# Splitting the eight PSUM banks two, four and two in a pairwise attention body

## The chip, the cores and the metric

One Trainium2 chip; the program runs on one core. The time is the device time of one execution, in microseconds (us). A core has TensorE (PE in the profile, its weight loads PEld), VectorE (DVE), ScalarE (ACT), GpSimd (POOL) and SyncE (SP), which each take their own instructions in order and meet at semaphores. TensorE writes its products to PSUM, which has eight banks of 128 partitions x 512 fp32 values.

## The reference, cut to what matters

The program is a four-layer network on x of 8 x 512 tokens x 256 features; each layer is an attention and a feed-forward part, each added to x. Three of the four attentions (layers 0, 2 and 3) have 16 heads of 16 features and use the code that is changed here. Layer 2 shows what is computed:

```python
q = (query @ Wq.T + bq).reshape(B, Tq, H, D).transpose(0, 2, 1, 3)
k = (key @ Wk.T + bk).reshape(B, Tk, H, D).transpose(0, 2, 1, 3)
v = (value @ Wv.T + bv).reshape(B, Tk, H, D).transpose(0, 2, 1, 3)
scores = jnp.einsum('bhqd,bhkd->bhqk', q, k) * SCALE
attn = jax.nn.softmax(scores, axis=-1)
out = jnp.einsum('bhqk,bhkd->bhqd', attn, v)
out = out.transpose(0, 2, 1, 3).reshape(B, Tq, C)
return out @ Wo.T + bo
```

Layer 0 has a mask that hides keys (an integer mask, 1 or 0), layer 3 a mask of floats that is added to the scores. Layer 1's attention and all feed-forward parts are other code, which the change leaves alone.

## The kernel before

The stages run one after another. `attention_by_pairs` makes one attention. It first projects queries, keys and values (`resident_projections`), and then runs the **body**, which the change is about. Tiles of the three attentions carry the same names in the profile (a_psA, a_psS, a_psZ, a_pT). The three bodies are called body 0, body 2 and body 3 below, by their layer.

The body works on pairs of heads. The two heads of a pair lie on partitions 0 to 63 and 64 to 127 of the stacks `qs` and `ks`; `par` is 0 or 1 and says which. There are 8 batches x 16 heads / 2 = 64 pairs, and a pair takes four steps, so a body has 256 steps (`QUARTERS`). A group is two pairs, 8 steps (`STEPS`); a batch is four groups, 32 steps. In each step t TensorE issues, in this order and by hand:

- body 0 only: two products of 512 columns that put the mask's term into the banks of `psS` (`hide_keys`, L1465, called H here);
- **A** (`maxima_scores`, L1455): the scores of 128 queries against all 512 keys, one product for each head of the pair, into `psA`. They are for step a = t + 16 (`LEAD`), two groups ahead. VectorE takes from each the largest score of each query (**R0** for par 0, then **R1** for par 1; L1663 in bodies 2 and 3, L1659 with a mask in body 0) and increments `a_used` with each;
- **S** (`exp_scores`, L1477): the scores the other way round, 128 keys by 512 queries, one product for each head, into `psS`. The maxima enter it as extra rows of the stack. ScalarE takes the exponential of each into `pT` (L1591) and increments `exp_done` with each;
- **Z** (`values`, L1492): pT times the values of the pair before, 8 instructions (16 records), into `psZ`;
- at some steps one piece of further work that uses a free bank of `psZ`: the transpose of the negated maxima (L1506, once in a group), four transposes of the finished heads (L1519, once in a group), four transposes of a batch's output (L1527, twice in a batch), a quarter of the output product (L1535, four times in a batch), and in body 0 eight products for masked rows (L1514, four times in a batch).

VectorE has two further duties among its reductions: `split_maxima` once in a group, and `take_output` once in a group, in the step after L1519, which it waits for before it goes on to R0 and R1 of that step.

The eight banks of PSUM are divided three, three and two: `psA`, `psS`, `psZ`. The products of `psA` and of `psS` use their three banks in rotation, by `unit(t, par)` = 2t + par, modulo 3. One wait stands ahead of each pair of products:

```python
if a >= 1:
    pe.wait_ge(a_used, 2 * a - 1)       # A: the pair starts when R0 of the step before is done
...
if t >= 1:
    pe.wait_ge(exp_done, 2 * t - 1)     # H and S: when the first exponential of the step before is done
```

Ahead of the 256 steps stand 16 steps with A alone, and the last 16 steps have no A.

Of the kernel before, what the change touches and what calls it, by code (L numbers as in the profile page):

```python
# [6 lines left out]
ACT = mybir.ActivationFunctionType  # L7
# [5 lines left out]
AX_X = mybir.AxisListType.X  # L13

P = 128
B = 8
S = 512
D = 256
N_TOK = B * S
TB = S // P  # L20
# [1007 lines left out]
HIDDEN = -1e30  # L1028
# [205 lines left out]
def attention_by_pairs(nc, A, G, nm, w, q_scale, hidden=None, added=None):  # L1234
# [9 lines left out]
    ring = 4 if hidden is not None else 5  # L1244
    with ExitStack() as ctx:
# [3 lines left out]
        psum = lambda n, s, d=F32: ctx.enter_context(nc.psum_tensor(nm + n, s, d))  # L1249
# [127 lines left out]
        mx = sb("mx", [P, 2, 2, 2, TB])  # L1377
# [3 lines left out]
        oh = sb("oh", [P, GH, P])  # L1381
        rden, on = sb("rden", [P, GH, TB]), sb("on", [P, 2, TB, D])
        oT, osb = sb("oT", [P, KD, S]), sb("osb", [P, 2, 2 * D])
        psA, psS, psZ = psum("psA", [P, 3, S]), psum("psS", [P, 3, S]), psum("psZ", [P, 2, S])
        a_ready, s_ready = [sem("a_ready0"), sem("a_ready1")], [sem("s_ready0"), sem("s_ready1")]
        a_used, max_ready, exp_done, o_done, oh_ready, rden_ready, x_full, x_free = (
            sem(n) for n in ("a_used", "max_ready", "exp_done", "o_done", "oh_ready", "rden_ready", "x_full", "x_free"))
# [32 lines left out]
        def unit(t, par):  # L1420
            return 2 * t + par

        with nc.Block() as block:
# [21 lines left out]
            def _(pe):  # L1445
                def maxima_scores(a):
                    p, q = a // TB, a % TB
                    g = p // 2
                    if a % STEPS == 0:
                        pe.wait_ge(group_loaded[g % ring], 16 * LOADS * (g // ring + 1))  # L1450
                    if a >= 1:
                        pe.wait_ge(a_used, 2 * a - 1)
                    for par in range(2):
                        r = slice(64 * par, 64 * par + max_row)
                        nc.tensor.matmul(psA[:, unit(a, par) % 3], qs[r, g % ring, p % 2, q * P:(q + 1) * P], ks[r, g % ring, p % 2],  # L1455
                                         start=True, stop=True).then_inc(a_ready[par], 1)

                def hide_keys(t):
                    u, kt = t // (TB * H // 2), t % TB
                    if t % (TB * H // 2) == 0:  # L1460
                        pe.wait_ge(hide_k_ready, u + 1)
                    if t >= 1:
                        pe.wait_ge(exp_done, 2 * t - 1)
                    for par in range(2):
                        nc.tensor.matmul(psS[:, unit(t, par) % 3], G.identb[:], hide_k[:, u % 2, kt, :], start=True, stop=False,  # L1465
                                         skip_group_check=True)

                def exp_scores(t):
                    p, kt = t // TB, t % TB
                    g = p // 2  # L1470
                    if t % STEPS == 0:
                        pe.wait_ge(max_stored[g % 2], 32 * (g // 2 + 1))
                    if t >= 1:
                        pe.wait_ge(exp_done, 2 * t - 1)
                    for par in range(2):
                        r = slice(64 * par, 64 * par + ROWS)
                        nc.tensor.matmul(psS[:, unit(t, par) % 3], ks[r, g % ring, p % 2, kt * P:(kt + 1) * P], qs[r, g % ring, p % 2],  # L1477
                                         start=(hidden is None), stop=True, skip_group_check=True).then_inc(s_ready[par], 1)

                def values(t):  # L1480
                    p, i = t // TB - 1, t % TB
                    g, par = p // 2, i // 2
                    b, j = g // NG, 2 * par + p % 2
                    if p % 2 == 0 and i == 0:
                        before = sum(1 for _, last, _, _ in found if last < t)
                        pe.wait_ge(x_free, before)
                        if g == 0:
                            pe.wait_ge(z_set, 1)
                    for kt in (2 * (i % 2), 2 * (i % 2) + 1):
                        pe.wait_ge(exp_done, unit(TB * p + kt, par) + 1)  # L1490
                        for q in range(TB):
                            last = nc.tensor.matmul(psZ[q * VP:q * VP + VW, g % 2, j * P:(j + 1) * P], V[:, b, kt, g % NG * GH + j, :],  # L1492
                                                    pT[:, p % 2, par, kt, q * P:(q + 1) * P], start=(kt == 0), stop=(kt == TB - 1),
                                                    skip_group_check=True)
                    if kt == TB - 1:
                        last.then_inc(o_done, 1)
# [57 lines left out]
            def _(act):  # L1554
                for t in steps:
# [29 lines left out]
                    if 0 <= t < QUARTERS:  # L1585
                        p, kt = t // TB, t % TB
                        for par in range(2):
                            act.wait_ge(s_ready[par], t + 1)
                            if p >= 2 and kt == 0:
                                act.wait_ge(o_done, 2 * (p - 2) + par + 1)  # L1590
                            nc.scalar.activation(pT[:, p % 2, par, kt, :], psS[:, unit(t, par) % 3], ACT.Exp).then_inc(exp_done, 1)  # L1591

            @block.vector
            def _(dve):
# [46 lines left out]
                for t in steps:  # L1641
                    if t % STEPS == 0 and 0 <= t // STEPS + 1 < GROUPS:
                        split_maxima(t // STEPS + 1)
                    for what, n, k in ending(t - 1, "heads"):
                        take_output(n, k)
                    a = t + LEAD
                    if a < QUARTERS:
                        p, q = a // TB, a % TB
                        b = p // 2 // NG
                        if hidden is not None and a % (TB * H // 2) == 0:  # L1650
                            dve.wait_ge(hide_q_ready, b + 1)
                        if hidden is not None and a % STEPS == 0 and a >= 2 * STEPS:
                            dve.wait_ge(e0_ready, a // STEPS - 1)
                        for par in range(2):
                            dve.wait_ge(a_ready[par], a + 1)
                            if hidden is not None:
                                if unit(a, par) >= 2:
                                    dve.wait_ge(a_used, unit(a, par) - 1)
                                nc.vector.tensor_tensor_reduce(  # L1659
                                    out=scored[:, par], in0=psA[:, unit(a, par) % 3], in1=hide_q[:, b % 2, q, :], scale=1.0, scalar=HIDDEN,  # L1660
                                    op0=ALU.add, op1=ALU.max, accum_out=mx[:, p // 2 % 2, par, p % 2, q:q + 1]).then_inc(a_used, 1)
                                continue
                            nc.vector.tensor_reduce(mx[:, p // 2 % 2, par, p % 2, q:q + 1], psA[:, unit(a, par) % 3], AX_X,  # L1663
                                                    ALU.max).then_inc(a_used, 1)

            @block.gpsimd
# [1384 lines left out]
```

## Time and profile before

| | before |
|---|---|
| time, median of 3 runs | 5270.98 us (5265.49 to 5279.82) |
| the profiled execution: time | 5273.62 us |
| its span | 5271.9 us |
| busy: PE, PEld, DVE, ACT, POOL | 4297.9, 3094.7, 3318.8, 2126.1, 808.5 us |
| steps of body 0, first to last S | 207.3 to 803.2 us |
| steps of body 2 | 3608.2 to 4003.6 us |
| steps of body 3 | 4589.7 to 4990.8 us |
| mean granted TensorE clock | 0.877 of full speed |

The span runs from the first to the last instruction in the trace; the time of that execution is 1.7 us more. Busy time of an engine is the time in which it executes; waits are not in it. The three bodies together take some 1,400 us of the span, about a quarter.

### The profile page before, as it was taken

The page shows a single profiled execution, that of the slowest core. Times are in us where ns is not written, and L with a number is a line of the kernel's source. Part 1 is how long each engine was busy: PE and PEld are TensorE (multiplying, and loading weights), DVE is VectorE, ACT ScalarE, POOL GpSimd, SP SyncE. Part 2 cuts the span into 40 slices and gives each one's busy share as a digit, 9 for nine tenths or more (in the row PEclk, how much of TensorE's full clock was granted, in tenths as well). Part 3 has the DMA queues.
Part 4 walks back from the last instruction along what each step waited for, and adds up shares of the span by engine and source line. Part 5 has one row for each costly group of instructions (what it writes and reads, how often), then busy time and mean ns, then how long its engine had stood idle before and what let it go on. Part 6 is the DMA issues. An engine that isn't in the chain of part 4 may idle for free. (4 is left out here: it accounts for less than half of the span.)

```text
span 5271.9 us, 86210 instructions
## 1 busy us (share of the span) xinstructions
PE 4297.9 (82%) x31622; PEld 3094.7 (59%) x31716; DVE 3318.8 (63%) x7267; ACT 2126.1 (40%) x3668; POOL 808.5 (15%) x478
## 2 busy tenths in 40 slices
PE   5699995999856999886278888667997988599999
PEld 4344444777745777665267777553554666355577
DVE  6466663444464666644864555367984888588687
ACT  2255552222212333342023433224775764277711
POOL 4423310000042000000012222221000333100000
PEclk8799997999967999988569999887997888699989
DMA  6222211000021000011033333441220003312100
GB/s 207 71 75 69 74 35 44 1 0 0 0 99 41 20 16 16 8 50 38 0 105 99 103 100 102 111 169 65 65 66 21 0 0 101 104 66 67 38 29 21
DMA packets 171769, 302.70 MB, mean 57 GB/s; under 512 B 22556, under 2 KB 90830, under 8 KB 171480
## 3 DMA queue, kind: packets, MB, share of 16 engines
q1 hardware_dynamic: 158824, 280.59, 16.8%
q0 software_dynamic: 12672, 18.42, 1.8%
q8 instruction: 177, 2.90, 0.2%
q14 instruction: 96, 0.79, 0.0%
HBM read 216.60 MB, written 80.77 MB: 56 GB/s over the span
## 5 line engine op out<-in xcount | busy, mean ns | idle before, releaser
L1591 ACT ACTIVATE a_pT<-a_psS 128x512 f32<-128x512 f32 x1536 | 835.9, 598 | 396.5 <-PE a_psS L1477 391.2
L1663 DVE TENSOR_REDUCE a_mx<-a_psA 128x1 f32<-128x512 f32 x1024 | 656.6, 685 | 81.8 <-PE a_psA L1455 81.6
L1455 PE MATMUL a_psA<-a_ks,a_qs 48*128 48x512 f32 (+1 forms) x1536 | 403.4, 521 | 158.8 <-PEq L46 95.3
L1492 PE MATMUL a_psZ<-a_pT,a_V 128*17 128x128 f32 x12288 | 487.3, 277 | 0.0
L1659 DVE CUSTOM_DVE_ANT_0 a_scored<-a_psA,a_hide_q 128x512 bf16<-128x512 f32 x512 | 332.6, 688 | 190.6 <-PE a_psA L1455 189.6
L1492 PEld LDWEIGHTS a_psZ<-a_pT,a_V 128*17 128x17 f32 x12288 | 272.2, 97 | 270.0 <-issue 159.1
L1455 PEld LDWEIGHTS a_psA<-a_ks,a_qs 48*128 48x128 f32 (+1 forms) x1536 | 151.0, 191 | 405.4 <-issue 176.3
L1477 PE MATMUL a_psS<-a_qs,a_ks 50*128 50x512 f32 (+1 forms) x1536 | 316.9, 406 | 2.7 <-ACT a_pT L1591 0.8
L2933 DVE SCALAR_TENSOR_TENSOR ex_h<-ex_psU,ex_ub,ex_sg 128x512 f32<-128x512 f32 x129 | 96.9, 751 | 318.0 <-PE ex_psU L159 311.0
L779 DVE TENSOR_TENSOR m_h_l<-m_h,m_h_h 128x512 fp32r<-128x512 f32 x64 | 44.3, 692 | 272.9 <-ACT m_h_h L723 270.7
L157 PE MATMUL m_psH<-m_xe_h,m_w_h 128*128 128x512 f32 x512 | 212.9, 416 | 0.0
L2888 ACT ACTIVATE ex_sg<-ex_psG,ex_gb 128x512 f32<-128x512 f32 x129 | 88.8, 689 | 294.2 <-PE ex_psG L159 291.5
L1675 POOL TENSOR_TENSOR X<-X,a_osb 128x512 f32<-128x512 f32 x48 | 61.3, 1281 | 936.7 <-ACT a_osb L1578 918.8
L159 PE MATMUL m_psH<-m_xe_h,m_w_l 128*128 128x512 f32 x512 | 203.7, 398 | 0.0
L158 PE MATMUL m_psH<-m_xe_l,m_w_h 128*128 128x512 f32 x512 | 203.6, 398 | 0.0
L2879 ACT CAST ex_w_h<-X 128x1024 fp32r<-128x1024 f32 x102 | 106.1, 1041 | 233.3 <-DMA X<-in_L_ffn_gw 230.3
L2813 POOL DMA_INDIRECT l1f_x<-ex_y,ex_idx_add x64 | 107.0, 1672 | 503.3 <-DVE ex_y L2970 488.7
L720 ACT ACTIVATE m_h<-m_psH 128x512 f32<-128x512 f32 x64 | 38.2, 598 | 349.9 <-PE m_psH L159 323.5
L1477 PEld LDWEIGHTS a_psS<-a_qs,a_ks 50*128 50x128 f32 (+1 forms) x1536 | 148.8, 189 | 18.7 <-ACT a_pT L1591 13.1
L1465 PE MATMUL a_psS<-a_hide_k,identb 128*128 128x512 bf16 x418 | 134.0, 384 | 28.1 <-ACT a_pT L1591 15.8
L903 PE MATMUL p_psY<-p_w,p_h 128*128 128x256 f32 x512 | 148.6, 430 | 0.3 <-ACT p_h L948 0.3
L965 POOL TENSOR_TENSOR p_drop<-p_g 128x512 f32<-128x512 f32 x65 | 105.5, 1624 | 270.3 <-ACT p_g L925 270.3
(557 smaller groups left out, 11144.2 us busy)
## 6 DMA issues: line engine op xcount, KB each, us to landing
a_k_parts<-a_p_kp SPq DMA_DIRECT2D x96, 256.0 KB
a_q_parts<-a_p_qp SPq DMA_DIRECT2D x96, 256.0 KB
a_qs<-a_q_parts SPq DMA_DIRECT2D x192, 128.0 KB
a_ks<-a_k_parts SPq DMA_DIRECT2D x192, 128.0 KB
X<-in_L_ffn_gw SPq DMA_DIRECT2D x36, 512.0 KB
X<-in_L_ffn_up_w SPq DMA_DIRECT2D x36, 512.0 KB
X<-in_L_ffn_down_w SPq DMA_DIRECT2D x36, 512.0 KB, 3.8
a_p_cT<-in_ctxT SPq DMA_DIRECT2D x24, 512.0 KB, 7.4
```

What stands on the lines that cost most here:

```text
L157: nc.tensor.matmul(out, wh, xh, start=start and n == 0, stop=False, **kw)
L158: nc.tensor.matmul(out, wh, xl, start=False, stop=False, **kw)
L159: last = nc.tensor.matmul(out, wl, xh, start=False, stop=stop and n == len(pairs) - 1, **kw)
L903: last = nc.tensor.matmul(out, h[:, m % 2, t * P:(t + 1) * P], w2[:, m, :], start=False, stop=(m == MF - 1), skip_group_check=True)
L1455: nc.tensor.matmul(psA[:, unit(a, par) % 3], qs[r, g % ring, p % 2, q * P:(q + 1) * P], ks[r, g % ring, p % 2], start=True, stop=True).the ...
L1465: nc.tensor.matmul(psS[:, unit(t, par) % 3], G.identb[:], hide_k[:, u % 2, kt, :], start=True, stop=False, skip_group_check=True)
L1477: nc.tensor.matmul(psS[:, unit(t, par) % 3], ks[r, g % ring, p % 2, kt * P:(kt + 1) * P], qs[r, g % ring, p % 2], start=(hidden is None), ...
L1492: last = nc.tensor.matmul(psZ[q * VP:q * VP + VW, g % 2, j * P:(j + 1) * P], V[:, b, kt, g % NG * GH + j, :], pT[:, p % 2, par, kt, q * P: ...
L1591: nc.scalar.activation(pT[:, p % 2, par, kt, :], psS[:, unit(t, par) % 3], ACT.Exp).then_inc(exp_done, 1)
L1659: nc.vector.tensor_tensor_reduce(out=scored[:, par], in0=psA[:, unit(a, par) % 3], in1=hide_q[:, b % 2, q, :], scale=1.0, scalar=HIDDEN, o ...
L1663: nc.vector.tensor_reduce(mx[:, p // 2 % 2, par, p % 2, q:q + 1], psA[:, unit(a, par) % 3], AX_X, ALU.max).then_inc(a_used, 1)
L2813: nc.gpsimd.indirect_dma_start(out=x_dram, out_offset=bass.IndirectOffsetOnAxis(idx_add[:, u, j:j + 1], 0), in_=y[:, u, j, :], in_offset=N ...
```

## The change

`psA` gets two banks, one for each head of the pair; `psS` gets four, two for each of two consecutive steps; `psZ` keeps its two. One exponential of 128 x 1024 (both heads of a pair) takes the place of two of 128 x 512. `exp_done` therefore counts steps and not units. The wait for the banks of `psS` is for the exponential two steps back. The wait for the banks of `psA` stands inside the loop over `par`: the first product waits for R0 of the step before, the second for R1 of the step before.

```diff
-        psA, psS, psZ = psum("psA", [P, 3, S]), psum("psS", [P, 3, S]), psum("psZ", [P, 2, S])
+        psA, psS, psZ = psum("psA", [P, 2, S]), psum("psS", [P, 4, S]), psum("psZ", [P, 2, S])
...
-                    if a >= 1:
-                        pe.wait_ge(a_used, 2 * a - 1)
                     for par in range(2):
+                        if a >= 1:
+                            pe.wait_ge(a_used, 2 * a - 1 + par)
                         r = slice(64 * par, 64 * par + max_row)
-                        nc.tensor.matmul(psA[:, unit(a, par) % 3], qs[r, g % ring, p % 2, q * P:(q + 1) * P], ks[r, g % ring, p % 2],
+                        nc.tensor.matmul(psA[:, par], qs[r, g % ring, p % 2, q * P:(q + 1) * P], ks[r, g % ring, p % 2],
                                          start=True, stop=True).then_inc(a_ready[par], 1)
...
-                    if t >= 1:
-                        pe.wait_ge(exp_done, 2 * t - 1)
+                    if t >= 2:
+                        pe.wait_ge(exp_done, t - 1)
                     for par in range(2):
-                        nc.tensor.matmul(psS[:, unit(t, par) % 3], G.identb[:], hide_k[:, u % 2, kt, :], start=True, stop=False,
+                        nc.tensor.matmul(psS[:, unit(t, par) % 4], G.identb[:], hide_k[:, u % 2, kt, :], start=True, stop=False,
...
-                    if t >= 1:
-                        pe.wait_ge(exp_done, 2 * t - 1)
+                    if t >= 2:
+                        pe.wait_ge(exp_done, t - 1)
...
-                        nc.tensor.matmul(psS[:, unit(t, par) % 3], ks[r, g % ring, p % 2, kt * P:(kt + 1) * P], qs[r, g % ring, p % 2],
+                        nc.tensor.matmul(psS[:, unit(t, par) % 4], ks[r, g % ring, p % 2, kt * P:(kt + 1) * P], qs[r, g % ring, p % 2],
...
-                        pe.wait_ge(exp_done, unit(TB * p + kt, par) + 1)
+                        pe.wait_ge(exp_done, TB * p + kt + 1)
...
                         for par in range(2):
                             act.wait_ge(s_ready[par], t + 1)
-                            if p >= 2 and kt == 0:
-                                act.wait_ge(o_done, 2 * (p - 2) + par + 1)
-                            nc.scalar.activation(pT[:, p % 2, par, kt, :], psS[:, unit(t, par) % 3], ACT.Exp).then_inc(exp_done, 1)
+                        if p >= 2 and kt == 0:
+                            act.wait_ge(o_done, 2 * (p - 2) + 2)
+                        nc.scalar.activation(pT[:, p % 2, :, kt, :], psS[:, 2 * (t % 2):2 * (t % 2) + 2], ACT.Exp).then_inc(exp_done, 1)
```

In VectorE's reductions `psA[:, unit(a, par) % 3]` becomes `psA[:, par]`, and nothing else.

## Rows read from the trace of the kernel before

**Rows 1.** Windows inside bodies 0 and 2: busy us (instructions) of each engine, clock, DMA.

```profile
240.00:780.00 540.00, 506.27 (x5442) 260.65 (x5529) 357.43 (x1099) 296.15 (x595) 160.37 (x97) 1.00 0.23 64
3640.00:3980.00 340.00, 333.36 (x4656) 182.82 (x4653) 304.26 (x547) 266.19 (x518) 15.37 (x12) 1.00 0.20 63
```

**Rows 2.** Instructions of tile psS, bodies 0 and 2: ns min/median/max, first and last start.

```profile
L1477 PEld LDWEIGHTS a_psS<-a_qs,a_ks x512: 182/187/335, 207.3 to 803.2; 50*128 50x128 f32 x171
...
L1477 PEld LDWEIGHTS a_psS<-a_qs,a_ks x512: 182/186/335, 3608.2 to 4003.6; 50*128 50x128 f32 x171
```

**Rows 3.** Timeline of body 2: start us, us, engine, instruction, [idle before <-releaser].

```profile
3799.39 3.24 DVE L1663 TENSOR_REDUCE a_mx<-a_psA 128x1 f32<-128x512 f32 x5
3799.53 0.50 PE L1455 MATMUL a_psA<-a_ks,a_qs 48*128 48x512 f32 x2
...
3800.81 0.50 PE L1455 MATMUL a_psA<-a_ks,a_qs 48*128 48x512 f32 x2
3801.15 0.39 PE L1477 MATMUL a_psS<-a_qs,a_ks 50*128 50x512 f32 x2
...
3801.47 0.63 PE L1492 MATMUL a_psZ<-a_pT,a_V 128*17 128x128 f32 x16
3802.03 0.66 PE L1519 MATMUL a_psZ<-ident,a_oh 128*128 128x128 f32 x4
3802.62 0.50 PE L1455 MATMUL a_psA<-a_ks,a_qs 48*128 48x512 f32 x2
...
3803.36 3.84 DVE L1663 TENSOR_REDUCE a_mx<-a_psA 128x1 f32<-128x512 f32 x6
...
3804.10 0.50 PE L1455 MATMUL a_psA<-a_ks,a_qs 48*128 48x512 f32 x2 [0.19 <-DVE a_mx L1663]
```

**Rows 4.** The costliest groups: line, engine, instruction, xcount | busy us, mean ns | idle before.

```profile
L1663 DVE TENSOR_REDUCE a_mx<-a_psA 128x1 f32<-128x512 f32 x1024 | 656.6, 685 | 81.8 <-PE a_psA L1455 81.6
```

**Rows 5.** Timeline of PE in body 2, steps with L1535 and L1506.

```profile
3830.08 0.50 PE L1455 MATMUL a_psA<-a_ks,a_qs 48*128 48x512 f32 x2
...
3832.36 0.50 PE L1455 MATMUL a_psA<-a_ks,a_qs 48*128 48x512 f32 x2
...
3833.84 0.50 PE L1455 MATMUL a_psA<-a_ks,a_qs 48*128 48x512 f32 x2
```

**Rows 6.** Timeline of body 0: a plain step, then the step after the heads' transposes.

```profile
452.15 0.50 PE L1455 MATMUL a_psA<-a_ks,a_qs 48*128 48x512 f32 x2
...
452.68 0.69 DVE L1659 CUSTOM_DVE_ANT_0 a_scored<-a_psA,a_hide_q 128x512 bf16<-128x512 f32 x1 [0.95 <-PE a_psA L1455]
...
452.92 1.08 ACT L1591 ACTIVATE a_pT<-a_psS 128x512 f32<-128x512 f32 x2 [0.51 <-PE a_psS L1477]
...
453.30 0.69 DVE L1659 CUSTOM_DVE_ANT_0 a_scored<-a_psA,a_hide_q 128x512 bf16<-128x512 f32 x1
453.57 0.11 PEld L1465 LDWEIGHTS a_psS<-a_hide_k,identb 128*128 128x128 bf16 x2 [0.40 <-ACT a_pT L1591]
...
454.11 0.51 PE L1455 MATMUL a_psA<-a_ks,a_qs 48*128 48x512 f32 x2
```

**Rows 7.** The same timeline, earlier.

```profile
428.35 0.50 PE L1455 MATMUL a_psA<-a_ks,a_qs 48*128 48x512 f32 x2
...
429.60 0.68 DVE L1659 CUSTOM_DVE_ANT_0 a_scored<-a_psA,a_hide_q 128x512 bf16<-128x512 f32 x1
...
430.35 0.50 PE L1455 MATMUL a_psA<-a_ks,a_qs 48*128 48x512 f32 x2
```

**Rows 8.** Timeline of PE at body 2's start: steps of A alone; two full steps.

```profile
3583.66 0.80 PE L1455 MATMUL a_psA<-a_ks,a_qs 48*128 48x512 f32 x2 [0.78 <-DVE a_mx L1663]
3585.24 0.80 PE L1455 MATMUL a_psA<-a_ks,a_qs 48*128 48x512 f32 x2 [0.78 <-DVE a_mx L1663]
...
3616.51 0.79 PE L1455 MATMUL a_psA<-a_ks,a_qs 48*128 48x512 f32 x2
...
3618.64 0.80 PE L1455 MATMUL a_psA<-a_ks,a_qs 48*128 48x512 f32 x2
```

More of the change, by code:

```diff
@@ L1659, in _ @@
                                 nc.vector.tensor_tensor_reduce(
-                                    out=scored[:, par], in0=psA[:, unit(a, par) % 3], in1=hide_q[:, b % 2, q, :], scale=1.0, scalar=HIDDEN,
+                                    out=scored[:, par], in0=psA[:, par], in1=hide_q[:, b % 2, q, :], scale=1.0, scalar=HIDDEN,
                                     op0=ALU.add, op1=ALU.max, accum_out=mx[:, p // 2 % 2, par, p % 2, q:q + 1]).then_inc(a_used, 1)
                                 continue
-                            nc.vector.tensor_reduce(mx[:, p // 2 % 2, par, p % 2, q:q + 1], psA[:, unit(a, par) % 3], AX_X,
+                            nc.vector.tensor_reduce(mx[:, p // 2 % 2, par, p % 2, q:q + 1], psA[:, par], AX_X,
                                                     ALU.max).then_inc(a_used, 1)
```

## The prediction, made before the changed kernel was run

> **What bounds the kernel now.** I read the windows first, since the change touches only the bodies. In [rows 1] the reader is to see that PE is the fullest engine in both bodies (506 of 540 us in body 0, 333 of 340 in body 2), that DVE is nearly as full in body 2 (304 of 340) but not in body 0 (357 of 540), that ACT is at 266 of 340 in body 2, and that PE's clock is granted in full (1.00). Next the places of the bodies [rows 2]: 256 steps take 596 us in body 0 (2.33 each) and 395 us in body 2 (1.54 each). Body 3 repeats body 2.
>
> Busy shares do not tell which wait ends last, so I went on to the timeline. In body 2 a plain step, from one A to the next, takes 1.28 us (3799.53 to 3800.81, [rows 3]), and three things ask for just that:
> - DVE: five reductions take 3.24 us, one of them 0.685 [rows 4], so they start every (3.24 - 0.685)/4 = 0.64 us, two in 1.28.
> - The round from A to R0 to the next A. A to the start of R0 is 0.53 us (452.15 to 452.68, [rows 6]); R0 takes 0.685; from its end to the next A pass 0.06 (3803.36 + 0.685 = 4.045 to 4.10, [rows 3]). Sum 1.275.
> - PE's own work. A to S 0.34, S to Z 0.32 (3800.81, 3801.15, 3801.47), Z to the next work 0.56 (3801.47 to 3802.03). Sum 1.22. I call this sum w.
>
> With a piece of further work w grows: with the heads' transposes to 1.81 (3800.81 to 3802.62), and L1527 is again four transposes; with L1535 2.28, with L1506 about 1.50 (3830.08, 3832.36, 3833.84 in [rows 5], where it is 1.48). In these steps PE is the bound. After the heads' transposes DVE does `take_output` ahead of R0, which starts at A + 0.74 and not 0.53 (3802.62 to 3803.36), so the next A comes after 1.48 (4.10). A batch of 32 steps has 10 plain steps, 4 with `take_output`, 4 with L1506, 6 with four transposes, 4 with L1535 and 4 more plain: 14 x 1.28 + 4 x 1.48 + 4 x 1.50 + 6 x 1.81 + 4 x 2.28 = 49.8 us, 1.56 a step, which agrees with 1.54 measured.
>
> In body 0 a plain step takes 1.96 (452.15 to 454.11, [rows 6]). Here w is 1.22 + 0.54 for H (453.57 to 454.11) = 1.76, and PE stands still for the rest: H waits for the first exponential of the step before (its weight loads sat idle for 0.40, released by ACT, of which 1.96 - 1.76 = 0.20 is standstill and the rest Z's products still running). That round is exponential to H 0.65, H to A 0.54, A to exponential 0.77: 1.96.
>
> **The change, part by part.**
>
> *Four banks for psS and the wait two steps back.* It takes away the round through ACT. In bodies 2 and 3 that round is not the bound (three others are met at 1.28), so nothing is gained there. In body 0 it is, and a plain step could fall to w, 1.76.
>
> *One exponential of 1024.* Two of 512 take 1.08 us together [rows 6]. The new one is not in the trace: at least 0.60 (one of the two), at most 2 x 0.60 = 1.20. Even 1.20 is hidden: S of step t now waits for the exponential of t - 2, which begins some 0.43 after its S (0.77 - 0.34) and so ends 1.63 after it, while two steps are 2.56. Cost 0. If that cover were gone, S would come late, then Z. The exponential starts only when both S are there, but they are released together already. Z at its latest reads the exponential of t - 2, for which S of step t has waited in either kernel: 0. `o_done` for par 1 of the pair before last is raised by Z of the step before, ahead of this S in PE's own order: 0.
>
> The Trainium skill (ScalarE: Activation LUTs, What ACT_TABLE_LOAD costs) gives 186 ns + 0.833 ns per column, an estimate of 1.04 us for 1024 columns; no row before has that shape.
>
> *Two banks for psA and the wait moved into the loop.* This is the part with a price. Before, both A start when R0 of the step before is done and run side by side (0.50 for the two). Now the second, A1, needs R1, which ends 0.64 later, and behind it in PE's order stand S, Z, the further work and the next A0. A0 may start earlier, ahead of A1 by d. Put A1 at 0. Then:
> - R0 starts at 0.53 - d, R1 0.64 later, ends 0.685 later, and 0.06 after that the next A1 may start: 1.915 - d. I call 1.915 the long round.
> - The next A0 comes at w, because PE is in order (S and Z wait behind A1). So the step P = max(w, 1.915 - d, 1.28), and the next d = P - w.
>
> Two steps in a row then take at least 1.915 + w. For plain steps that is 3.135, 1.57 each in place of 1.28: they alternate between 1.915 and 1.28. After a step bound by PE (d = 0) the next plain step takes 1.915. With `take_output` the long round is 1.915 + 0.21 = 2.125. Walking through the 32 steps of a batch (L1506 at 0, 8, 16, 24; four transposes at 4, 6, 9, 12, 20, 28; `take_output` at 5, 13, 21, 29; L1535 at 14, 15, 17, 18) gives from step 0:
> 1.50, 1.915, 1.28, 1.855, 1.81, 2.125, 1.81, 1.915 | 1.50, 1.915, 1.81, 1.325, 1.81, 2.125, 2.28, 2.28 | 1.915, 2.28, 2.28, 1.915, 1.81, 2.125, 1.28, 1.855 | 1.50, 1.915, 1.28, 1.855, 1.81, 2.125, 1.28, 1.855: sum 58.3 against 49.8. That is +8.5 a batch; 240 of the 256 steps have both A and S, so 7.5 batches: **+64 us in body 2, +64 in body 3.**
>
> In body 0 the long round is 0.53 + 0.62 (R0 to R1, 452.68 to 453.30) + 0.69 + 0.06 = 1.90. Against w = 1.76, d stays small. Of the 10 plain steps 9 take 1.90 and one 1.76 (the second of two without further work at 10 and 11): 18.9 for 19.6. In the four steps with `take_output` R0 starts at A + 1.25 (428.35 to 429.60, [rows 7]) and the step takes 2.00 now (430.35), because A waits for R0 alone; with R1 it is 1.25 + 0.62 + 0.69 + 0.06 = 2.62: 10.5 for 8.0. The others are PE's and stay. Sum +1.8 a batch, x 7.5: **+13 us in body 0.**
>
> The 16 steps ahead, of A alone, take 1.57 each at the lower clock [rows 8], which is the round A to R0 to A (0.80 + 0.77). A0 and A1 each keep such a round of their own, half a step apart: 0. The last 16 steps have no A: 0. No DMA and no POOL work is moved.
>
> Bounds for what no row shows, how S and Z follow an A1 that runs alone. The nearest row has the pair and 0.34 to S, and A1 and the second S use the same partitions, so I take 0.34. At the least S follows at 0.10, with all but that hidden beside A1 (w = 0.98): the walk gives +33 a body, and 0 for body 0. At the most the further waits cost 0.10 a step (w = 1.32): +77 a body and +26. Totals: +66 to +180.
>
> **The rivals.**
> - *The clock falls.* A regular standstill of PE in each step could lower the granted clock. At the lower level a full step is 2.13 of PE work (3616.51 to 3618.64, [rows 8]) and the long round 1.57 + 0.64 = 2.21, so 2.17 a plain step and not 1.57: +0.60 x 240 = +144 in each of two bodies, 5702 us in all. Against it: body 0 stands still for 0.20 in a plain step of 1.96, and its clock is 1.00 [rows 1]; here it would be 0.35 in 1.57, more, but never longer than 0.7 at a time. The Trainium skill (TensorE: Matmul & The Clock Gate, A second HAM failure mode: psum-queue depth-cycling) warns of just such small idles between groups of matmuls; by it the sum would be this rival's, and the trace of body 0, with smaller ones, disagrees.
> - *Faster: A1's wait costs nothing, and only body 0's wait for ACT goes.* The mechanism: A1 finds R1 done. That decides from w <= 0.645 in bodies 2 and 3 (1.915 + w <= 2 x 1.28). Then body 0's 10 plain steps gain 0.20 each: 2.0 x 7.5 = -15, 5256 us. PE's S and Z alone take 0.88 in [rows 3], so it needs a wrong reading of the round.
> - *Only a part*: R1 is done sooner than I reckon or S hides beside A1 still more, so that +20 to +66 is left, some 5320 us.
> - That the change does nothing: the sums of both signs would have to cancel; within the cases above.
>
> **How the numbers follow.** The profiled execution took 5273.6 us, 2.6 above the median. 5273.6 + 64 + 64 + 13 = 5414.6; taking off some of the 2.6 I say 5414. Chance of this forecast (+66 to +180) 0.79, of the part 0.08, the clock 0.07, faster 0.06. The range is that of the bounds, 5273.6 + 66 = 5340 to 5454, with a few us more at each end: 5335 to 5460. Slower by over 0.3% (16 us, about what a measurement of this kernel can tell from no change): 0.92; within: 0.03; faster: 0.05.
>
> **What would show it.** Body 2 and 3 last some 460 us from first to last S, body 0 some 610. In body 2 A is no longer one row x2: A1 starts 0 to 0.7 after A0, with PE's idle ahead of it released by DVE L1663; plain steps alternate near 1.9 and 1.28; DVE's busy share falls from 0.89 to about 0.76. In body 0 the idle ahead of H released by ACT is gone, and one ahead of A released by L1659 has come. The clock stays at 1.00. I am wrong if A0 to A1 to S shows less than 0.34 behind a late A1, if the clock falls, or if ACT's exponential is waited for.

## The result: 2.35% slower

The changed kernel takes 5395.6 us (median of 4 runs, 5388.08 to 5402.18) against 5270.2 before (the median of 4 runs, with the one made beside the changed kernel): a ratio of 1.0235, 95% interval 1.0214 to 1.0256. The forecast was 5414, with a range of 5335 to 5460. The profiled execution of the changed kernel has a span of 5397.1 us, 125.2 more than before, at a mean granted clock of 0.878 (0.877 before).

The windows of the changed kernel, with the columns of [rows 1]:

```profile
240.00:780.00 540.00, 523.06 (x5391) 270.55 (x5384) 347.52 (x1077) 275.64 (x359) 159.06 (x96) 0.99 0.23 64
3660.00:4050.00 390.00, 378.88 (x4629) 201.10 (x4627) 302.79 (x543) 253.42 (x298) 15.28 (x12) 1.00 0.19 55
```

PE still looks full in body 2, 379 of 390 us, and its clock is still granted in full there; in body 0 it is 0.99 in the mean. What has fallen is the work done per time: 4629 products in 390 us are 11.9 a microsecond, before it was 4656 in 340, 13.7. DVE went from 0.89 to 0.78 busy in body 2. PE's busy share hides the loss, since two products of A that ran side by side now run one after the other and count twice; the page says so in the group of L1455, 403.4 us busy before for the same 1536 products:

```profile
L1591 ACT ACTIVATE a_pT<-a_psS 128x1024 f32<-128x1024 f32 x768 | 786.6, 1025 | 528.8 <-PE a_psS L1477 527.1
L1663 DVE TENSOR_REDUCE a_mx<-a_psA 128x1 f32<-128x512 f32 x1024 | 658.2, 685 | 165.3 <-PE a_psA L1455 160.7
L1455 PE MATMUL a_psA<-a_ks,a_qs 48*128 48x512 f32 (+1 forms) x1536 | 570.2, 519 | 151.3 <-PEq L46 97.1
```

The places of the bodies, as in [rows 2], for bodies 0, 2 and 3:

```profile
L1477 PEld LDWEIGHTS a_psS<-a_qs,a_ks x512: 182/186/335, 209.9 to 816.6; 50*128 50x128 f32 x171
...
L1477 PEld LDWEIGHTS a_psS<-a_qs,a_ks x512: 182/186/335, 3626.7 to 4077.5; 50*128 50x128 f32 x171
...
L1477 PEld LDWEIGHTS a_psS<-a_qs,a_ks x512: 182/186/335, 4664.8 to 5115.2; 52*128 52x128 f32 x171
```

From first to last S that is 606.7, 450.8 and 450.4 us, against 595.9, 395.4 and 401.1: +10.8, +55.4 and +49.3, 115.5 of the 125.2 us. The rest is 2.6 us ahead of body 0, 5.1 between bodies 0 and 2, 1.2 between bodies 2 and 3 and 0.8 behind. The largest of these, 2810.1 us for 2805.0, is almost all code that no kernel here changes, and it took 2801.6 (e8) to 2814.9 us (e3) in the other kernels, so it is no more than executions differ.

Body 2's timeline of PE, plain steps, to hold against [rows 3]:

```profile
3728.16 0.63 PE L1455 MATMUL a_psA<-a_ks,a_qs 48*128 48x512 f32 x2
3728.49 0.52 PE L1477 MATMUL a_psS<-a_qs,a_ks 50*128 50x512 f32 x2
3728.95 0.63 PE L1492 MATMUL a_psZ<-a_pT,a_V 128*17 128x128 f32 x16
3729.51 1.02 PE L1455 MATMUL a_psA<-a_ks,a_qs 48*128 48x512 f32 x2
3730.03 0.73 PE L1477 MATMUL a_psS<-a_qs,a_ks 50*128 50x512 f32 x2
3730.69 0.63 PE L1492 MATMUL a_psZ<-a_pT,a_V 128*17 128x128 f32 x16
3731.26 0.62 PE L1455 MATMUL a_psA<-a_ks,a_qs 48*128 48x512 f32 x2
```

One product of A takes 0.50. A row "x2" of 1.02 therefore means that the second began 1.02 - 0.50 = 0.52 after the first; a row of 0.62 means 0.12. A1 thus starts at 3728.29, 3730.03 and 3731.38: steps of 1.74 and 1.35, 3.09 for the two, where two steps took 2.56. What A1 waits for stands at its weight load, in the timeline of all engines:

```profile
3730.03 0.18 PEld L1455 LDWEIGHTS a_psA<-a_ks,a_qs 48*128 48x128 f32 x1 [0.34 <-DVE a_mx L1663]
```

Z follows A1 by 0.66, however late A1 is, and the next A0 follows Z by 0.56 and waits for nothing. The time is lost between A0 and A1, where PE has A0 alone to run and so hardly ever counts as idle. S behind a late A1 does not look as it did: its first product starts with A1, at 3730.03, on the half of the partitions that A0 has left, and only the second follows A1 by 0.34 (3730.03 + 0.73 - 0.39 = 3730.37). Z stands behind the second, so the step is no shorter for it.

The step with `take_output`, of the same timeline:

```profile
3820.46 0.49 PE L1455 MATMUL a_psA<-a_ks,a_qs 48*128 48x512 f32 x2
...
3821.20 2.57 DVE L1663 TENSOR_REDUCE a_mx<-a_psA 128x1 f32<-128x512 f32 x4
...
3821.94 1.10 PE L1455 MATMUL a_psA<-a_ks,a_qs 48*128 48x512 f32 x2 [0.18 <-DVE a_mx L1663]
```

R0 starts 0.74 after A as before, and A0 follows its end at 3821.94 as before, but A1 waits until 3821.94 + 0.60 = 3822.54: 2.08 for 1.48. In body 0 the same step:

```profile
455.20 0.50 PE L1455 MATMUL a_psA<-a_ks,a_qs 48*128 48x512 f32 x2
455.54 0.40 PE L1477 MATMUL a_psS<-a_qs,a_ks 50*128 50x512 f32 x2
455.87 0.63 PE L1492 MATMUL a_psZ<-a_pT,a_V 128*17 128x128 f32 x16
456.43 0.60 PE L1465 MATMUL a_psS<-a_hide_k,identb 128*128 128x512 bf16 x2
457.20 1.10 PE L1455 MATMUL a_psA<-a_ks,a_qs 48*128 48x512 f32 x2 [0.17 <-DVE a_mx L1659]
```

H follows Z by 0.56 with no wait for ACT: that gain came. A1 starts at 457.20 + 0.60 = 457.80, 2.60 after the last, for 2.0 before.

### The profile page after: what moved, and what is told of

The parts are those of the page before. It is cut to its first block and busy times, and to the rows that moved or that the text cites. A ratio compares the mean times of both kernels' runs of the same rounds, so it can differ in the third digit from the quotient of the medians.

```text
span 5397.1 us, 85932 instructions
## 1 busy us (share of the span) xinstructions
PE 4462.2 (83%) x31716; PEld 3170.4 (59%) x31716; DVE 3319.0 (61%) x7267; ACT 2083.9 (39%) x2900; POOL 808.2 (15%) x478
## 5 line engine op out<-in xcount | busy, mean ns | idle before, releaser
L1591 ACT ACTIVATE a_pT<-a_psS 128x1024 f32<-128x1024 f32 x768 | 786.6, 1025 | 528.8 <-PE a_psS L1477 527.1
L1455 PE MATMUL a_psA<-a_ks,a_qs 48*128 48x512 f32 (+1 forms) x1536 | 570.2, 519 | 151.3 <-PEq L46 97.1
L1455 PEld LDWEIGHTS a_psA<-a_ks,a_qs 48*128 48x128 f32 (+1 forms) x1536 | 229.2, 191 | 478.6 <-issue 217.5
L1477 PE MATMUL a_psS<-a_qs,a_ks 50*128 50x512 f32 (+1 forms) x1536 | 416.9, 421 | 0.0
L1477 PEld LDWEIGHTS a_psS<-a_qs,a_ks 50*128 50x128 f32 (+1 forms) x1536 | 187.3, 188 | 13.9 <-issue 11.1
L1465 PE MATMUL a_psS<-a_hide_k,identb 128*128 128x512 bf16 x512 | 154.5, 384 | 0.0
```

The costliest lines, as they stand in the source:

```text
L1455: nc.tensor.matmul(psA[:, par], qs[r, g % ring, p % 2, q * P:(q + 1) * P], ks[r, g % ring, p % 2], start=True, stop=True).then_inc(a_ready ...
L1465: nc.tensor.matmul(psS[:, unit(t, par) % 4], G.identb[:], hide_k[:, u % 2, kt, :], start=True, stop=False, skip_group_check=True)
L1477: nc.tensor.matmul(psS[:, unit(t, par) % 4], ks[r, g % ring, p % 2, kt * P:(kt + 1) * P], qs[r, g % ring, p % 2], start=(hidden is None), ...
L1591: nc.scalar.activation(pT[:, p % 2, :, kt, :], psS[:, 2 * (t % 2):2 * (t % 2) + 2], ACT.Exp).then_inc(exp_done, 1)
```

## The experiments

Nine more kernels ran. Of each body the table has the time from first to last S in the profiled execution.

| kernel | median us | before beside it | ratio (95%) | body 0 | body 2 | body 3 |
|---|---|---|---|---|---|---|
| before | 5270.2 | | | 595.9 | 395.4 | 401.1 |
| changed | 5395.6 | 5270.2 | 1.0235 (1.0214 to 1.0256) | 606.7 | 450.8 | 450.4 |
| e1 banks of A alone | 5409.6 | 5276.4 | 1.0253 (1.0224 to 1.0283) | 609.2 | 455.9 | 452.0 |
| e2 two exponentials | 5390.8 | 5276.4 | 1.0218 (1.0201 to 1.0235) | 603.3 | 451.9 | 451.6 |
| e3 pair waits for R1 | 5523.3 | 5276.4 | 1.0452 (1.0420 to 1.0484) | 606.6 | 508.5 | 498.4 |
| e4 A1 behind Z | 5400.9 | 5276.4 | 1.0238 (1.0219 to 1.0256) | 625.3 | 446.4 | 448.3 |
| e5 H behind A | 5331.6 | 5277.4 | 1.0108 (1.0093 to 1.0123) | 649.1 | 394.4 | 405.8 |
| e6 three banks, two waits | 5268.1 | 5277.4 | 0.9981 (0.9969 to 0.9992) | 596.3 | 391.3 | 399.2 |
| e7 changed in body 0 alone | 5287.4 | 5277.4 | 1.0017 (1.0007 to 1.0027) | 610.6 | 400.8 | 395.9 |
| e8 two waits everywhere | 5257.4 | 5280.6 | 0.9951 (0.9936 to 0.9967) | 583.3 | 390.2 | 399.5 |
| e9 four banks of A | 5363.9 | 5280.6 | 1.0142 (1.0121 to 1.0163) | 627.1 | 426.4 | 427.5 |

In e7 bodies 2 and 3 run the old code and take 400.8 and 395.9: one execution's body is known to some 5 us. The granted clock goes with part of this spread. Behind its first steps, body 3 of the kernel before has one window of 20 us in which the clock is 0.74, and e7's body 3 has none:

```profile
4740.00:4760.00 20.00, 19.75 (x232) 10.07 (x232) 14.17 (x25) 13.27 (x26) 0.00 (x0) 0.74 0.18 61
```

Against the 395.9 of e7 the changed kernel's body 3 is longer by 54.5 us and not by 49.3, nearly as much as body 2 (55.4).

**e1, the banks of A alone.**

```diff
-        psA, psS, psZ = psum("psA", [P, 3, S]), psum("psS", [P, 3, S]), psum("psZ", [P, 2, S])
+        psA, psS, psZ = psum("psA", [P, 2, S]), psum("psS", [P, 3, S]), psum("psZ", [P, 2, S])
...
-                    if a >= 1:
-                        pe.wait_ge(a_used, 2 * a - 1)
                     for par in range(2):
+                        if a >= 1:
+                            pe.wait_ge(a_used, 2 * a - 1 + par)
```

As in the change, `psA[:, unit(a, par) % 3]` is `psA[:, par]`.

> The kernel before with one part of the change: psA gets two banks, with a wait ahead of each product; psS keeps three banks and two exponentials. My theory, that the wait for R1 ahead of the second product is the whole loss: bodies 2 and 3 as in the changed kernel (450 us from first to last S each), body 0 longer than there, since its wait for the exponential stays: plain steps 1.96, the step with take_output 2.6 for 2.0, so 596 + 0.6 x 4 x 7.5 = 614 us. In all 5271 + 55 + 49 + 18 + 8 = about 5400 us (5390 to 5410). The rival, that the joined exponential and the waits for it cost the time: 5271 us.

5409.6 us, bodies 2 and 3 456 and 452 us, body 0 609 for the 614 expected. The whole loss is there without the wider exponential and without the four banks of psS. The loss is that of psA's part.

**e2, two exponentials.** The changed kernel, with this and the counts of `exp_done` to fit:

```diff
-                        nc.scalar.activation(pT[:, p % 2, :, kt, :], psS[:, 2 * (t % 2):2 * (t % 2) + 2], ACT.Exp).then_inc(exp_done, 1)
+                            nc.scalar.activation(pT[:, p % 2, par, kt, :], psS[:, unit(t, par) % 4], ACT.Exp).then_inc(exp_done, 1)
```

> The changed kernel with two exponentials of 512 again, in the four banks of psS, each waiting for its own product. My theory: ACT is on no path, so 5396 us as the changed kernel (5388 to 5404), with ACT busy some 50 us more. The rival, that the joined exponential costs the time: back towards 5271, at least 20 us below the changed kernel.

5390.8 us. The page's group of the exponentials in this run:

```profile
L1591 ACT ACTIVATE a_pT<-a_psS 128x512 f32<-128x512 f32 x1536 | 832.9, 595 | 496.9 <-PE a_psS L1477 488.0
```

ACT is busy 46 us more than in the changed kernel and the time is not longer. The joined exponential is worth nothing here, in either direction: it is hidden.

**e3, the pair waits for R1.** The changed kernel, with one wait ahead of both A:

```diff
-                    for par in range(2):
-                        if a >= 1:
-                            pe.wait_ge(a_used, 2 * a - 1 + par)
+                    if a >= 1:
+                        pe.wait_ge(a_used, 2 * a)
+                    for par in range(2):
```

> The changed kernel with one wait ahead of both products of A, for R1 of the step before, so that they start together again. My theory, that the round A to R1 to A sets the step: every step of bodies 2 and 3 takes max(w, 1.88), with take_output 2.09; a batch takes 24 x 1.88 + 4 x 2.09 + 4 x 2.29 = 62.6 us against 57.9 in the changed kernel, + 36 us a body; body 0 nearly as in the changed kernel. About 5468 us (5455 to 5480). The rival, that the loss comes from the two products of A no longer running side by side: they do again, so 5271 to 5330 us.

5523.3 us, more than either theory gave. The rival is out: the two A run side by side again, and the kernel is slower by another 128 us. Its timeline of PE in body 2:

```profile
3850.07 0.51 PE L1455 MATMUL a_psA<-a_ks,a_qs 48*128 48x512 f32 x2
...
3851.95 0.50 PE L1455 MATMUL a_psA<-a_ks,a_qs 48*128 48x512 f32 x2 [0.58 <-DVE a_mx L1663]
```

A plain step is 1.88, the round A to R1 to A, and PE stands idle for 0.58 of it. A batch with no disturbance (from the A of the step with a batch's first L1535, at 3858.54, to the next such A, at 3921.01) takes 62.5 us; 62.6 was expected. What was not expected is in the windows of this run:

```profile
3780.00:3820.00 40.00, 33.32 (x431) 17.92 (x431) 27.82 (x49) 24.05 (x30) 2.54 (x2) 0.96 0.19 52
3820.00:3860.00 40.00, 37.16 (x395) 18.71 (x386) 25.97 (x47) 21.16 (x25) 0.00 (x0) 0.69 0.16 48
3860.00:3900.00 40.00, 31.70 (x427) 16.80 (x426) 28.35 (x51) 23.40 (x28) 2.54 (x2) 1.00 0.17 48
...
3820.00:3840.00 20.00, 19.94 (x181) 9.62 (x171) 11.74 (x21) 9.56 (x11) 0.00 (x0) 0.50 0.15 46
```

The granted clock falls to its lower level in some places (0.69 in the mean of one window, and 0.50 in the first half of it); there PE looks busier and issues fewer products. That is the prediction's rival of the clock, but in a kernel where PE has nothing at all to run for 0.58 of each plain step; in the changed one A0 runs in that time. Against the changed kernel bodies 2 and 3 are longer by 57.7 and 48.0; what of it lies above the 36 that the waits alone were reckoned at I put down to these falls, without a run that parts the two.

**e4, A1 behind Z.** The changed kernel, with another order in a step (the conditions between the calls are cut, the comments added):

```diff
-                        maxima_scores(t + LEAD)            # A0, A1
-                        exp_scores(t)                      # S0, S1
-                        values(t)                          # Z
+                        maxima_scores(t + LEAD, (0,))      # A0
+                        exp_scores(t, (1,))                # S1
+                        values(t)                          # Z
+                        maxima_scores(t + LEAD, (1,))      # A1
+                        exp_scores(t, (0,))                # S0
```

> The changed kernel with PE's order in a step changed and nothing else: (H), A of par 0, S of par 1, Z, A of par 1, S of par 0, further work. Each A still has a product on the other half of the partitions beside it, and the second A no longer has S and Z behind it. My theory: the second A comes 0.90 us after the first, when R1 of the step before is done; plain steps of bodies 2 and 3 take (0.90 + 1.87) / 2 = 1.39, a batch 51.5 us (50.2 before, 57.9 changed), + 9 us a body over the kernel before; in body 0 plain steps fall to w = 1.77 and those with take_output to 2.0, 14 us below before. About 5275 us (5260 to 5300). The rival, that the banks or the joined exponential themselves cost: near 5396.

5400.9 us: the expectation fell. From its timeline of PE in body 2:

```profile
3830.83 0.63 PE L1492 MATMUL a_psZ<-a_pT,a_V 128*17 128x128 f32 x16
...
3831.39 0.50 PE L1455 MATMUL a_psA<-a_ks,a_qs 48*128 48x512 f32 x1
...
3831.82 1.13 PE L1535 MATMUL a_psZ<-a_wo,a_oT 128*128 128x256 f32 x4
```

The waits did what they should: plain steps of body 2 alternate between 1.28 and 1.60 from Z to Z, and some 130 steps without further work take 1.44 in the mean, for 1.72 in the changed kernel counted alike. But a pair of products on half the partitions that stands alone takes 0.43 until a product on all of them can start (3831.39 to 3831.82), where A and S one behind the other take 0.66 for both. So w rose by 0.20: steps with L1535 take 2.48 for 2.29. Steps with L1519 take up to 2.48 (2.40 in the mean) for 1.82, more than w explains; S0 now comes late in the step, so the exponential and the copy of the heads behind it on ACT do too, and L1519 waits for that copy, as the same run's timeline of PE and ACT shows:

```profile
3797.55 1.02 ACT L1595 ACTIVATE a_pT<-a_psS 128x1024 f32<-128x1024 f32 x1 [0.56 <-PE a_psS L1477]
...
3798.48 0.58 ACT L1588 COPY a_oh<-a_psZ 128x512 f32<-128x512 f32 x1
...
3799.20 0.63 PE L1519 MATMUL a_psZ<-ident,a_oh 128*128 128x128 f32 x4 [0.42 <-ACT a_oh L1588]
```

The exponential had waited 0.56 for S0, the copy behind it ends at 3799.06, and L1519 begins at 3799.20 after a wait of 0.42. In bodies 2 and 3 the other steps lost nearly all that the plain ones gained (446.4 and 448.3 us for 450.8 and 450.4), and body 0 lost 18.6 us more: there too a step with further work is longer by 0.20 (with L1527 2.45 for 2.25). The total is no test of the banks, then, but the plain steps are: with the same two banks of `psA` and the same waits, and only the order changed, they fell from 1.72 to 1.44. My price for w was right only for the order that it was read from.

**e5, H behind A.** The kernel before, with H after A in body 0:

```diff
-                        hide_keys(t)
-                        maxima_scores(t + LEAD)
+                        maxima_scores(t + LEAD)
+                        hide_keys(t)
```

> The kernel before with the order of body 0 changed from H, A, S, Z to A, H, S, Z, banks as before. A then runs while H waits for the exponential. My theory of body 0: the round through ACT is exponential to H 0.65, H to S 0.54, S to exponential 0.43 = 1.62, below w, so plain steps fall from 1.96 to 1.77; those with take_output stay at 2.0 by the round A to R0 to A. 10 x 0.19 x 7.5 = 14 us less than before, about 5257 against 5271; body 0 some 582 us from first to last S for 596. If instead plain steps are PE's own work and the wait is cover, no difference.

5331.6 us and not 5257, body 0 53 us longer. The same mistake, seen more plainly, in this run's timeline of PE in body 0:

```profile
482.25 0.50 PE L1455 MATMUL a_psA<-a_ks,a_qs 48*128 48x512 f32 x2
482.69 0.60 PE L1465 MATMUL a_psS<-a_hide_k,identb 128*128 128x512 bf16 x2
483.22 0.51 PE L1477 MATMUL a_psS<-a_qs,a_ks 50*128 50x512 f32 x2
483.66 0.63 PE L1492 MATMUL a_psZ<-a_pT,a_V 128*17 128x128 f32 x16
```

A to H 0.44, H to S 0.53, S to Z 0.44, and Z to the next product on all partitions or to A 0.56: w = 1.97 for 1.76. H, on all partitions, stands between A and S and parts them, in every step. Plain steps hardly show it, since the wait held them at 1.96 before: 1.97 now. The loss lies in the steps with further work, which PE itself bounds: they gain the 0.21 and another 0.09, because A and not H now follows the further work (four transposes to A 0.58, to H 0.49 before). Steps with L1519 take 2.55 for 2.25, those with L1514 3.99 for 3.69.

**e6, three banks with two waits.** The kernel before, with:

```diff
-                    if a >= 1:
-                        pe.wait_ge(a_used, 2 * a - 1)
                     for par in range(2):
+                        if a >= 1:
+                            pe.wait_ge(a_used, 2 * a - 2 + par)
```

> The kernel before with its wait for psA moved into the loop, as in the change, but with three banks: the first product of A waits for R1 of two steps back, the second for R0 of the step before. My theory, that what matters is which reduction the second product waits for: nothing is lost, since the second waits as it did and the first may start earlier; 5255 to 5275 us. The rival, that two waits in the loop and products that start apart cost the time: near the 5396 of the changed kernel.

5268.1 us, ratio 0.9981: no loss, a small gain. It has the change's waits in the loop, and its products may start apart. What differs from e1 is the third bank, and with it the reductions that are waited for: the second product waits for R0 of the step before, and not for R1. So neither two waits nor products that start apart cost the time. That the two banks cost nothing by themselves no run shows alone, since two banks need the later wait; but in e4 the plain steps fell with those very banks.

**e7, the changed layout in body 0 alone** (3, 3, 2 and the old waits where there is no integer mask).

> The changed layout (two, four, two; one exponential) in body 0 alone, the old one in bodies 2 and 3. My theory: body 0 is 607 us from first to last S, as in the changed kernel, 11 us more than before, bodies 2 and 3 are 395 and 401 as before; 5271 + 11 = about 5283 us (5276 to 5292). If the gain and the loss in body 0 are mis-sized, or the body costs differently by what follows it, it falls outside.

5287.4 us, ratio 1.0017, some 9 us slower than before; body 0 610.6 us, with the clock between 0.83 and 0.93 in four windows of 20 us behind 260 us. Body 0 alone loses a little, as reckoned; nearly all is lost in bodies 2 and 3.

**e8, two waits everywhere.** e6, with this in H and in S:

```diff
-                    if t >= 1:
-                        pe.wait_ge(exp_done, 2 * t - 1)
                     for par in range(2):
+                        if t >= 1:
+                            pe.wait_ge(exp_done, 2 * t - 2 + par)
```

> Banks three, three, two and two exponentials, as before, but every wait for a bank stands ahead of the product that needs it: A as in the run with three banks and two waits; H and S of par 0 wait for the second exponential of two steps back, those of par 1 for the first of the step before. In body 0 the first H then runs while the second waits, and the round through ACT is exponential to second H 0.65, to A 0.27, to exponential 0.77 = 1.69, below w = 1.76. My theory: plain steps of body 0 fall to w, 10 x 0.19 x 7.5 = 14 us; bodies 2 and 3 as in the run with three banks and two waits. About 5254 us against 5270 (ratio 0.9955). If the time that H gives back is not on the path, 0.998 as that run.

5257.4 us, ratio 0.9951 (0.9936 to 0.9967), the fastest of all. Its timeline of PE in body 0:

```profile
453.41 0.50 PE L1455 MATMUL a_psA<-a_ks,a_qs 48*128 48x512 f32 x2
...
454.63 0.60 PE L1465 MATMUL a_psS<-a_hide_k,identb 128*128 128x512 bf16 x2
455.16 0.50 PE L1455 MATMUL a_psA<-a_ks,a_qs 48*128 48x512 f32 x2
...
455.50 0.39 PE L1477 MATMUL a_psS<-a_qs,a_ks 50*128 50x512 f32 x2
```

This step began with A at 453.41 and ended with A at 455.16: 1.75, for 1.96. Body 0 takes 583.3 us, 12.6 less than before. What the prediction hoped for from the change's psS part in body 0, plain steps at w, is had with three banks, by waits that are no earlier than they must be.

**e9, four banks of A.** The mirror: psA four banks and a wait two steps back (`a_used`, 2a - 2), psS two, two exponentials, and

```diff
+                        if t >= 1:
+                            pe.wait_ge(exp_done, 2 * t - 1 + par)
```

> The mirror of the change: psA four banks with a wait two steps back, psS two banks with a wait ahead of each product, two exponentials. My theory says that a pair of banks with a wait ahead of each costs where the second consumer of the pair ends late: here the second exponential, S to its end 0.43 + 1.08, + 0.05, a long round of 1.56 against 1.87 for the maxima. Plain steps of bodies 2 and 3 take (1.56 + 1.22) / 2 = 1.39 for 1.28, a batch 52.5 us (50.2 before), + 17 us a body; in body 0 the long round is 2.17 and the plain step (2.17 + 1.76) / 2 = 1.97, as before, after the long steps more, + 17. About 5271 + 51 = 5322 us (5290 to 5345), between before and the changed kernel. A rival that blames VectorE alone says 5271 or less.

5363.9 us, outside 5290 to 5345: the sign and the place are right, the size is not. Beside the kernel before it is 83 us slower, and 51 was expected. In body 2:

```profile
3842.88 0.51 PE L1455 MATMUL a_psA<-a_ks,a_qs 48*128 48x512 f32 x2
...
3843.22 0.84 PE L1477 MATMUL a_psS<-a_qs,a_ks 50*128 50x512 f32 x2
3843.56 0.18 PEld L1477 LDWEIGHTS a_psS<-a_qs,a_ks 50*128 50x128 f32 x1 [0.30 <-ACT a_pT L1591]
...
3843.99 0.63 PE L1492 MATMUL a_psZ<-a_pT,a_V 128*17 128x128 f32 x16
```

S0 comes 0.34 after A, S1 (its weight load is the PEld row) another 0.34 later, when ACT has released it, and Z 0.77 after S0 in place of 0.32: an S1 that starts apart stands alone ahead of Z, and pays 0.43 as in e4. In body 0, from the same run:

```profile
471.27 0.88 PE L1465 MATMUL a_psS<-a_hide_k,identb 128*128 128x512 bf16 x2
472.08 0.49 PE L1455 MATMUL a_psA<-a_ks,a_qs 48*128 48x512 f32 x2
...
473.50 0.88 PE L1465 MATMUL a_psS<-a_hide_k,identb 128*128 128x512 bf16 x2
```

the step is 2.23, the long round itself and not its mean with w: both S stand behind the second H, so an earlier first H lets no exponential start earlier.

## Why the prediction held, point by point

- *Bodies 2 and 3 are bound by three things at 1.28.* Borne out in part: plain steps take 1.28 before, and the shorter ones of the changed kernel 1.28 too. w itself shows in e9, where A waits for the reductions of two steps back:

```profile
3844.55 0.50 PE L1455 MATMUL a_psA<-a_ks,a_qs 48*128 48x512 f32 x2
...
3845.78 0.50 PE L1455 MATMUL a_psA<-a_ks,a_qs 48*128 48x512 f32 x2
```

That step of body 2 is 1.23, and w was put at 1.22. DVE's pace and the round A to R0 to A are not parted by any run.
- *Four banks for psS give nothing in bodies 2 and 3, and in body 0 free H of its wait.* Shown for body 0: the wait is gone from its timeline, and e8, which takes the same wait away by other means, is 12.6 us shorter there. For bodies 2 and 3, e1 loses as much there without the four banks.
- *The joined exponential costs nothing.* Shown by e2. It lasts 1.025 us (bounds given: 0.60 to 1.20); with the Trainium skill's formula (ScalarE: Activation LUTs, What ACT_TABLE_LOAD costs) the estimate was 1.04, and the row agrees.
- *A1 waits for R1, and S, Z and the next A0 wait behind A1.* Shown by e1, e6, the plain steps of e4 and the timeline. The walk through the batch came out nearly step by step: from A1 at 3682.25 (the step with L1506) the trace has 1.63, 1.74, 1.36, 1.74, 1.82, 2.07, 1.82, 1.87 for 1.50, 1.915, 1.28, 1.855, 1.81, 2.125, 1.81, 1.915.
- *The size.* The forecast was +141 us in the profiled execution, +125 came. The term that was too large is the long round, 1.915: it measures 1.87. Of its parts the distance from R0 to R1 is too long. I took 0.64 from a stretch of five reductions without a pause; in a pair that begins after a wait of DVE it is 1.29 - 0.685 = 0.605:

```profile
3731.79 1.29 DVE L1663 TENSOR_REDUCE a_mx<-a_psA 128x1 f32<-128x512 f32 x2 [0.46 <-PE a_psA L1455]
```

With 1.88 for it the two plain steps are 3.10; 3.09 was measured. The 32 steps from the A1 of the step with a batch's first L1535, at 3706.78, to the next such, at 3764.64, take 57.9 us (58.3 reckoned), and before, from A to A, 3677.06 to 3727.31, they took 50.2 (49.8 reckoned): + 7.6 and not + 8.5, x 7.5 = 57 us a body, where 55 and 49 were measured (54.5 for body 3 beside an old body 3 without the low clock). In the steps with L1506 the two short instructions of `split_maxima` hold R0 back as well, which I had left out: 1.62 for 1.50.
- *Body 0: + 13.* 10.8 measured, 14.7 in e7, both with falls of the clock in them (see the rivals). Two of the reckoned steps are seen: 2.60 with `take_output` (2.62 reckoned), and 1.90 for the median step without further work, from Z to Z (1.90 reckoned).
- *The rivals.* In bodies 2 and 3, where the rival of the clock was priced, the clock did not fall behind the first 20 us (1.00 in every later window), though in e3, where PE stands still 0.58 in each 1.88, it did. In body 0 it fell a little, which was named as a sign of being wrong:

```profile
400.00:440.00 40.00, 38.46 (x372) 20.48 (x370) 24.48 (x76) 19.24 (x26) 15.75 (x14) 0.96 0.25 67
```

There, and from 480 to 520 us (0.96), the kernel before has 1.00. The eight products for masked rows in this window, and the same products of the kernel before, in the timelines of PE:

```profile
417.69 3.79 PE L1514 MATMUL a_psZ<-a_V,a_is_hidden 128*128 128x272 f32 x8
```

and before:

```profile
412.12 2.10 PE L1514 MATMUL a_psZ<-a_V,a_is_hidden 128*128 128x272 f32 x8
```

From Z to Z three such steps took 5.10, 5.38 and 5.33 us (starting at 261.1, 417.1 and 496.2), where the median is 3.69 and no such step of the kernel before is over 4.1: together 4.7 us of the body's +10.8. Without them it would be some 6 us, an estimate, where 13 was reckoned; that the body's sum came so near is partly luck. Faster, and no change: not found.
- *A sign that came and changed nothing.* The prediction was to be wrong if S showed less than 0.34 behind a late A1. Its first product does start with A1; the sum holds because Z stands behind the second product, which is the one on A1's partitions. Nor does PE show an idle ahead of A1, as was foretold: A0 covers it, and the wait stands at the weight load.
- *A sum that holds for one order alone:* w as a sum of 0.34, 0.32, 0.56 and 0.54 holds for this order alone. The change leaves the order alone; e4 and e5 did not.

e1 is at 5410 and the changed kernel at 5396, but each has its own runs of the kernel before beside it (5276 and 5270), and the intervals of the two ratios overlap: that they differ is not shown. Not settled is how much of e3's further loss is the clock's, and why body 0, without its falls of the clock, loses less than was reckoned.

## What to carry to other kernels

Count banks by the consumer that ends last before the next product may start, not by how many buffers a tile has: three banks in rotation let both products of a pair start behind the first reduction, two make the second wait for the last, and whatever stands behind it in the queue waits too. Place a wait ahead of the very product that needs it and no earlier; that gave here, with the old banks, what the new ones were to bring in body 0 (12.6 us). When two consumers are slow in turn, add the whole round (product, reduction of one, reduction of the other, wake-up) and take its mean with the engine's own work. The mean holds only where the earlier first product lets its consumer start earlier; in e9's body 0 it does not, and the step is the whole round.

## What the runs showed of the hardware that was not expected

- Two pairs of products on half the partitions cost 0.66 us until a product on all of them may start when they follow one another (A, S), and 0.43 each when something on all partitions stands between: 0.20 more a step (e4, e5).
- TensorE's granted clock fell in e3 to a mean of 0.69 in a window of 40 us, and to 0.50, the lower level of 1.2 GHz, in the first 20 us of it; around the fall plain steps have PE busy for 1.3 of 1.88 us. In bodies 2 and 3 of the changed kernel, where about 0.5 of every second plain step has A0 alone and PE hardly any idle time, it stayed at 1.00 behind their first 20 us. The Trainium skill (TensorE: Matmul & The Clock Gate, A second HAM failure mode: psum-queue depth-cycling) tells of a kernel that cycles through PSUM banks, in which the short idles of PE between groups of matmuls let the clock swing between its two levels; the trace of e3 agrees, bodies 2 and 3 of the changed kernel do not show it.
- The clock can also fall in one execution and not in another of the same code: body 3, in its old code, has 20 us at a mean of 0.74 in the kernel before and none such in e7, and takes 401.1 and 395.9 us. In body 0 of the changed kernel three steps with L1514 took 5.10 to 5.38 us; in e1, with the same two banks of `psA`, all of them took 3.68 to 3.70.
- A busy share of PE rose (0.82 to 0.83 of the span, and 0.94 to 0.97 in body 0's window) while its work per time fell: of two products side by side the profile counts the time once.
